# Thirty-six expert steps for thirty-nine: eight of them shared by two experts on two column halves of the array

## The chip, the core and the metric

The kernel runs on one core of one Trainium2 chip. The metric is the device time of the program in microseconds. The engines are named PE (TensorE), DVE (VectorE), ACT (ScalarE), POOL (GpSimd) and SP (SyncE); PEld is TensorE's weight load.

## The reference

Two layers over 4 batches of 512 tokens of 512 numbers (f32). The first quantizes to int8 levels, multiplies, gates and multiplies again, batch by batch, and adds the result to x. The second is a mixture of 8 experts, each token going to the two that its router scores highest:

```python
x = x + _L0_xattn_ref(_layernorm(x, axis=-1), fside_BxS2xS2_0, ctx_1024)
x = x + _L0_ffn_ref(_layernorm(x, axis=-1), L0_ffn_router_w, ...)

scores = jnp.einsum('btd,de->bte', x, router_w)
routing_weights, routing_idx = jax.lax.top_k(jax.nn.softmax(scores, axis=-1), 2)
routing_weights = routing_weights / jnp.sum(routing_weights, axis=-1, keepdims=True)
...
gate = jnp.einsum('bted,edf->btef', dispatched, gate_proj)      # 512 -> 256
up = jnp.einsum('bted,edf->btef', dispatched, up_proj)          # 512 -> 256
act = jax.nn.silu(gate) * up
expert_out = jnp.einsum('btef,efd->bted', act, down_proj)       # 256 -> 512
return jnp.einsum('bted,bte->btd', expert_out, combine_weights)
```

2048 tokens with two picks are 4096 rows for the experts. With the inputs drawn, the reference picks the experts 0 to 7 for 537, 487, 492, 519, 516, 531, 512 and 502 rows.

## The kernel before

The first layer runs batch by batch, its steps interleaved by tables of steps, one table for each engine (`SP_ORDER`, `POOL_ORDER`, `DVE_ORDER`, `ACT_ORDER`, `PE_ORDER`). An engine works its table off strictly in order; semaphores hold it where an operand is missing. Meanwhile the experts' weights are loaded and split into a 16-bit high part and a 16-bit rest ("high" on ScalarE, "low" on GpSimd), and stay on the chip for all eight experts.

The second layer sorts the 4096 rows by expert into tiles of 128 rows. VectorE chooses, ranks and makes one-hot matrices ("choose", "place"); TensorE applies them ("sort", "table"). "list" (`list_tiles`, L907) works out, with small operations that each wait for the one before (`then`, L807), how many tiles each expert owns and where they start; "indices" (`compact` on TensorE L1289, `indices` on VectorE L943) turns this into the rows to gather and to scatter, the expert of each tile and, in `scatter_after`, the number of tiles that must have landed before it. This happens twice: after batches 0 and 1 for nine early tiles that are certainly full (`EARLY`), and after the last batch for the rest (`MOST` = 30). 39 tiles are made because 4096 rows on eight experts can need that many; tiles without a row are computed too.

One expert step i is, by engine:

- GpSimd gathers 128 token rows with an indirect DMA ("gather", L666), four tiles ahead for the late tiles.
- TensorE transposes them ("x low", L1313), ScalarE takes the f16 high part (L1104), VectorE the rest (L970).
- TensorE multiplies with the expert's gate and up weights in three passes: 12 matmuls, cut in two parts of six ("up first", "up rest", L1328). ScalarE applies silu (L1111), VectorE multiplies (L978).
- TensorE transposes again ("a low", L1339), ScalarE and VectorE evict (L1118, L988), TensorE multiplies with the down weights: six matmuls ("take y" on TensorE, L1349), and ScalarE evicts with the row's weight ("take y" on ScalarE, L1133).
- GpSimd adds the 128 rows to the output in memory with an indirect DMA ("scatter", L687).

A matmul of the experts has 128 columns of weights (the tile's rows) and streams 512 numbers of an expert's weights. From step 11 on the orders are made by a loop: on TensorE x low i + 1, up first i, a low i - 1, up rest i, take y i - 1.

A token's two experts are two additions to one row, which must not be in flight together. So a scatter of an early tile waits for the one before (L679). A late one loads `scatter_after`, waits for the semaphore `landed` and does a one-column operation (`hold`, L288): it waits until all tiles of earlier experts have landed, not for those of its own. SP counts `landed` up as the scatters land, in order (L517 to L521). On GpSimd's queue, gather i + 4 stands in front of one scatter, or of two at every third i; scatters 3 to 8 are still to be done when the late part begins. ScalarE's take y i writes into the buffer of tile i - 8 and waits for its landing (L1131).

`keep_busy` (L1164) issues matmuls whose result nobody reads in the first layer; `IN_STRIPS` cuts some of them into two or four column strips of the array.

## Time and profile before

| | us |
|---|---|
| median of three runs | 383.36 |
| the three runs | 381.07, 383.36, 383.91 |
| the profiled execution | 381.06, span 379.3 |
| PE busy / DVE / ACT / POOL | 321.9 / 225.1 / 202.9 / 244.5 |

The span runs from the first to the last instruction of the profiled execution; its own time is 1.76 us more. The granted clock of TensorE was 0.993 of full speed over the span. The late expert steps run from about 223 us on; the last one ends at 370 us, and its rows land after that. Times in the rows are counted from the span's start.

### The profile page before, as it was taken

The numbers are of one execution on the slowest core, as the hardware profiler recorded it, in microseconds if no ns is written. First come the engines' busy times: TensorE is split into PE (matmuls) and PEld (weight loads), VectorE is DVE, ScalarE is ACT, GpSimd is POOL, SyncE is SP. The second block draws the span as 40 slices with busy tenths as digits, with TensorE's granted clock in tenths as the row PEclk, the third lists the DMA queues.
The fourth block names the chain that finished last, engine by engine and source line by source line (L and its number), as shares of the span: only waits on it lengthen the run. The fifth ranks groups of instructions, "written<-read, shape, count | busy, mean of one in ns | idle before, by whom it ended". The sixth has DMA issues, their size and how long they took to land.

```text
span 379.3 us, 6450 instructions
## 1 busy us (share of the span) xinstructions
PE 321.9 (85%) x1955; PEld 189.8 (50%) x1955; DVE 225.1 (59%) x515; ACT 202.9 (54%) x382; POOL 244.5 (64%) x271
## 2 busy tenths in 40 slices
PE   4698757877798885679899899999999999999980
PEld 1455435545665652375574455555555555555530
DVE  3588887879899988878678732333333333333320
ACT  1557568888897796139635234444444444444430
POOL 6486697879999971685461472656667746675441
PEclk9999999999999999999999999999999999999997
DMA  7765446745765508147127554557687657786544
GB/s 247 245 264 196 136 163 199 265 147 165 277 258 188 189 35 242 64 167 232 75 31 275 86 144 80 101 99 116 129 137 115 125 95 123 132 137 107 92 55 55
DMA packets 27551, 56.79 MB, mean 150 GB/s; under 512 B 2624, under 2 KB 13888, under 8 KB 25600
## 3 DMA queue, kind: packets, MB, share of 16 engines
q0 software_dynamic: 8736, 20.45, 29.9%
q1 hardware_dynamic: 17968, 35.39, 27.0%
q10 hardware_dynamic: 816, 0.54, 0.5%
q8 instruction: 18, 0.29, 0.3%
q14 instruction: 13, 0.11, 0.1%
HBM read 37.50 MB, written 18.87 MB: 149 GB/s over the span
## 4 chain that ended last, share of the span: by engine, by line
PE 33%; POOL 22%; issue 17%; DVE 14%; ACT 5%; DMA 4%; POOLq 2%; SPq 0%; DVEq 0%; ACTq 0%
PE bank_h L1328 13%; PE bank_q L1349 6%; POOL x L648 4%; POOL w_in L666 3%; POOL out L687 3%; DVE amax L726 3%; PE bank_t L1313 3%; PE bank_q L1194 2%; POOL w_in L619 2%; POOL gu_lo L584 2%; DVE rmax L756 2%; POOLq L682 2%; PE bank_h L1222 2%; ACT xn L1014 2%; DMA stage<-tokens,gather_at 2%
## 5 line engine op out<-in xcount | busy, mean ns | idle before, releaser
L1328 PE MATMUL bank_h<-gu_hi,xT 128*128 x312 | 103.9, 379 | 0.0
L1328 PE MATMUL bank_h<-gu_lo,xT 128*128 x156 | 59.1, 379 | 0.0
L970 DVE SCALAR_TENSOR_TENSOR xT<-bank_t,xT 128x512 f16<-128x512 f32 x39 | 26.8, 689 | 53.9 <-ACT xT L1104 53.8
L1349 PE MATMUL bank_q<-dn_hi,aT 128*128 x156 | 52.6, 379 | 1.7 <-DVE aT L988 1.4
L1328 PEld LDWEIGHTS bank_h<-gu_hi,xT 128*128 128x128 f16 x312 | 30.5, 98 | 29.3 <-issue 0.2
L666 POOL DMA_INDIRECT w_in<-tokens,gather_at x30 | 29.8, 993 | 17.8 <-issue 7.6
L584 POOL TENSOR_TENSOR gu_lo<-stage,gu_hi 128x1024 bf16<-128x1024 f32 x16 | 34.0, 2135 | 7.5 <-ACT gu_hi L1061 7.3
L978 DVE SCALAR_TENSOR_TENSOR gated<-bank_h,gated 128x256 f32<-128x256 f32 x39 | 16.5, 422 | 32.0 <-ACT gated L1111 32.0
L1111 ACT ACTIVATE gated<-bank_h 128x256 f32<-128x256 f32 x39 | 14.9, 383 | 38.0 <-PE bank_h L1328 38.0
L726 DVE TENSOR_REDUCE amax<-bank_t 128x1 f32<-128x512 f32 x48 | 30.8, 684 | 6.6 <-PE bank_t L1194 4.7
L687 POOL DMA_INDIRECT out<-h,scatter_at x17 | 26.9, 1580 | 11.8 <-DMA out<-h,scatter_at 4.5
L687 POOL DMA_INDIRECT out<-xn,scatter_at x16 | 25.2, 1575 | 11.6 <-ACT xn L1133 9.7
L1349 PE MATMUL bank_q<-dn_lo,aT 128*128 x78 | 29.6, 379 | 0.0
L1118 ACT ACTIVATE aT<-bank_r 128x256 f16<-128x256 f32 x39 | 14.8, 383 | 27.0 <-PE bank_r L1339 25.8
L988 DVE TENSOR_TENSOR aT<-bank_r,aT 128x256 f16<-128x256 f32 x39 | 16.3, 422 | 20.4 <-ACT aT L1118 20.4
L1104 ACT ACTIVATE xT<-bank_t 128x512 f16<-128x512 f32 x39 | 23.0, 591 | 9.2 <-PE bank_t L1313 8.9
L1349 PEld LDWEIGHTS bank_q<-dn_hi,aT 128*128 128x128 f16 x156 | 15.2, 97 | 21.8 <-issue 8.1
L288 POOL TENSOR_TENSOR hold_p<-identf 128x1 f32<-128x1 f32 x30 | 11.1, 372 | 21.0 <-SPq L521 18.5
L648 POOL TENSOR_TENSOR x<-x,xn 128x512 f32<-128x512 f32 x16 | 19.9, 1284 | 4.2 <-DVE xn L802 4.1
L1328 PEld LDWEIGHTS bank_h<-gu_lo,xT 128*128 128x128 f16 x156 | 15.3, 98 | 11.4
L1133 ACT ACTIVATE h<-bank_q,slot_weight 128x512 f32<-128x512 f32 x17 | 11.7, 687 | 15.1 <-PE bank_q L1349 15.1
L619 POOL TENSOR_TENSOR w_in<-w_in,row_s 128x1024 f32<-128x1024 f32 x8 | 17.3, 2184 | 3.0 <-ACT row_s L1027 2.9
(197 smaller groups left out, 704.5 us busy)
## 6 DMA issues: line engine op xcount, KB each, us to landing
stage<-in_L_ffn_gate_proj SPq DMA_DIRECT2D x8, 512.0 KB, 4.2
stage<-in_L_ffn_up_proj SPq DMA_DIRECT2D x8, 512.0 KB, 4.1
stage<-in_L_ffn_down_proj SPq DMA_DIRECT2D x8, 512.0 KB, 4.9
x<-in_x SPq DMA_DIRECT2D x4, 1024.0 KB, 6.3
out<-x SPq DMA_DIRECT2D x4, 1024.0 KB, 4.6
tokens<-xn SPq DMA_DIRECT2D x4, 1024.0 KB, 4.5
x_in<-in_x SPq DMA_DIRECT2D x3, 1024.0 KB, 7.5
w_in<-in_fside_BxS2xS SPq DMA_DIRECT2D x3, 1024.0 KB, 5.6
```

The costliest lines, as they stand in the source:

```text
L584: pool.tensor_tensor(lo, staged(k), hi, ALU.subtract).then_inc(sem("lo_done"), 1)
L619: pool.tensor_tensor(rows, rows, spread(row_s1[:], [P, J // 2, D], 1), ALU.mult).then_inc(sem("ws_ready"), 1)
L648: pool.tensor_tensor(x1[:, j], x1[:, j], xn2[:, j], ALU.add).then_inc(sem("x1_ready"), 1)
L666: pool.indirect_dma_start(out=xg(i), out_offset=None, in_=rows, in_offset=bass.IndirectOffsetOnAxis(ap=gather_at[:, i:i + 1], axis=0)).the ...
L687: pool.indirect_dma_start(out=out, out_offset=bass.IndirectOffsetOnAxis(ap=scatter_at[:, i:i + 1], axis=0), in_=y(i), in_offset=None, comp ...
L726: dve.tensor_reduce(amax[which][:, b % 2, side, c, 0:1], bank, AX.X, ALU.max, apply_absolute_value=True).then_inc(ring_t.taken, 1)
L970: dve.scalar_tensor_tensor(out=xT[i % 2][:, 1].rearrange("p c t -> p (c t)"), in0=bank, scalar=X_SCALE, in1=xT[i % 2][:, 0].rearrange("p c ...
L978: dve.scalar_tensor_tensor(out=gated[i % 2][:], in0=bank[:, F:2 * F], scalar=A_SCALE / X_SCALE, in1=gated[i % 2][:], op0=ALU.mult, op1=ALU ...
L988: dve.tensor_tensor(aT[i % 2][:, 1].rearrange("p c t -> p (c t)"), bank[:, 0:F], aT[i % 2][:, 0].rearrange("p c t -> p (c t)"), ALU.subtra ...
L1104: act.activation(xT[i % 2][:, 0].rearrange("p c t -> p (c t)"), bank, ACT.Copy, scale=X_SCALE).then_inc(sem("x_high"), 1)
L1328: ins = pe.matmul(bank, xT[i % 2][:, part, c], rhs[:, cols], start=(c == 0 and m == 0), stop=(c == C - 1 and m == 2))
L1349: ins = pe.matmul(bank, aT[i % 2][:, part, c], rhs[:, cols], start=(c == 0 and n == 0), stop=(c == FC - 1 and n == 2))
```

## The change

The tiles are now counted in halves of 64 rows. Each expert's rows make `halves` = whole halves (count / 64, rounded down) and a rest of 0 to 63 rows. Two whole halves make a full tile; there are places for 28 of them, 9 early and 19 late (`WHOLE`, `FULL`). Eight mixed tiles, steps 15 to 22 (`MIXED_FROM`), have two halves each. The high half of mixed tile k belongs to expert k and holds its rest. The low half holds expert k's odd whole half, if it has one; otherwise it is free, and the halves of full tiles beyond the 28 are put into the free ones ("spilled"). In all 36 steps.

- TensorE: in a mixed step each of the 18 matmuls becomes two, on 64 columns of weights: the low one with the expert's weights at an address in a register, the high one with expert k's at a fixed address. They write partitions 0 to 63 and 64 to 127 of one bank.
- GpSimd: a mixed tile is scattered in two DMAs of 64 rows. `scatter` of the low half waits until every unit before has landed, by a constant. `scatter_high` loads `high_after` and waits for what `scatter` k waited for, and for the low half also, where that holds a spilled half. Late full tiles behind step 22 wait at least for all mixed units. There are 19 + 16 = 35 late units (`UNITS`); two steps of three take two scatters from the list instead of one of three. The semaphores of the landings are 16 instead of 8.
- VectorE: "list" has three operations more, "indices" one; new are "halves 0" (nine), "mixed list 0" (eleven) and "mixed indices 0" (twelve), and on TensorE "mixed indices 0" (16 small matmuls).
- `share` is one column, broadcast; a few more constants are made at the start by GpSimd.

```diff
+HALF = P // 2
+MIXED_FROM = 15
+FAR = 4096.0
...
 DVE_ORDER
-    "place 2, x low 6, up 5, table 2, list 1, x low 7, indices 1, up 6, a low 4, a low 5, up 7, a low 6, x low 8, "
-    "x low 9, x low 10, up 8, up 9, a low 7, a low 8, up 10, a low 9")
+    "place 2, x low 6, up 5, table 2, list 1, x low 7, indices 1, halves 0, up 6, a low 4, a low 5, mixed list 0, up 7, a low 6, x low 8, "
+    "mixed indices 0, x low 9, x low 10, up 8, up 9, a low 7, a low 8, up 10, a low 9")
 PE_ORDER
-    "indices 1, x low 8, a low 5, up first 7, up rest 7, take y 4, a low 6, take y 5, x low 9, up first 8, "
+    "indices 1, x low 8, a low 5, up first 7, up rest 7, mixed indices 0, take y 4, a low 6, take y 5, x low 9, up first 8, "
...
-    TILES = (N * TOPK + E * (P - 1)) // P
+    MIXED = E
+    WHOLE = (N * TOPK // HALF - MIXED) // 2
+    TILES = WHOLE + MIXED
+    MIXED_END = MIXED_FROM + MIXED
+    UNITS = TILES - EARLY + MIXED
+    FULL = WHOLE - EARLY
+    AHEAD = MIXED_FROM - EARLY
...
-        to_scatter = waiting + [("scatter", i) for i in range(EARLY, TILES)]
+        to_scatter = waiting[:]
+        for i in range(EARLY, TILES):
+            to_scatter.append(("scatter", i))
+            if MIXED_FROM <= i < MIXED_END:
+                to_scatter.append(("scatter high", i))
...
-            for _ in range(2 if to_scatter[0] not in waiting and i % 3 == 0 else 1):
+            for _ in range(2 if to_scatter[0] not in waiting and i % 3 != 1 else 1):
...
+        def units_upto(i):
+            return 1 + i + 1 - EARLY + min(max(i + 1 - MIXED_FROM, 0), MIXED)
+        def unit(i, half=0):
+            return units_upto(i - 1) - 1 + half
...
             def scatter(i):
...
-                    before = pool.value_load(scatter_after[0:1, i:i + 1], min_val=1, max_val=MOST)
+                elif phase == 1:
+                    before = pool.value_load(scatter_after[0:1, i:i + 1], min_val=1, max_val=1 + UNITS)
                     pool.wait_ge(sem("landed"), before)
                     hold(pool, i)
+                else:
+                    pool.wait_ge(sem("landed"), 1 + unit(i))
                 ring_q.emptied(pool, "take y", 0, i)
+                if phase < 2:
+                    add_rows(i, 0, y(i), scatter_at[:, i:i + 1])
+                else:
+                    add_rows(i, 0, y(i)[0:HALF], scatter_at[0:HALF, i:i + 1])
+            def scatter_high(i):
+                k = i - MIXED_FROM
+                before = pool.value_load(high_after[0:1, k:k + 1], min_val=1, max_val=1 + UNITS)
+                pool.wait_ge(sem("landed"), before)
+                hold(pool, i)
+                add_rows(i, 1, y(i)[HALF:P], high_at[0:HALF, k:k + 1])
...
             def gate_up(half, i):
...
+                        if phase_of[i] < 2:
+                            ins = pe.matmul(bank, xT[i % 2][:, part, c], rhs[:, cols], start=start, stop=stop)
+                        else:
+                            pe.matmul(bank[0:HALF], xT[i % 2][:, part, c, 0:HALF], rhs[:, cols], start=start, stop=stop)
+                            own = (gu_hi, gu_lo, gu_hi)[m][:, i - MIXED_FROM, c]
+                            ins = pe.matmul(bank[HALF:P], xT[i % 2][:, part, c, HALF:P], own, start=start, stop=stop)
...
             def take_y(i):
...
-                        act.wait_ge(sem("landed"), before - EARLY + 2)
+                        act.wait_ge(sem("landed"), units_upto(before))
```

On GpSimd's queue (POOL), in the late expert steps, a gather and a scatter stood like this before; `w_in` is the gather's buffer, `h` the scatter's, `[waits ...]` names semaphores:

```order
L666 DMA w_in<-tokens,gather_at 128x512 [waits t_filled]
L682 TENSOR_LOAD scatter_after
L682 ISA x2
L288 TENSOR_TENSOR hold_p<-identf 128x1 [waits landed]
L687 DMA out<-h,scatter_at 7168x512 [waits q_taken]
```

Now, from the gather in front of the low half of step 16 to the one behind its high half:

```order
L707 DMA w_in<-tokens,gather_at 128x512 [waits t_filled]
L713 DMA out<-h,scatter_at 7168x512 [waits q_taken,landed]
L741 TENSOR_LOAD high_after
L741 ISA x2
L314 TENSOR_TENSOR hold_p<-identf 128x1 [waits landed]
L713 DMA out<-h,high_at 7168x512
```

A mixed step puts two scatters into the queue, and the first waits for `landed` itself, with a constant, before the next gather can be issued.

On TensorE (PE), between up rest 7 and take y 4, nothing stood before:

```order
L1328 MATMUL bank_h<-gu_lo,xT 128x512
L1328 MATMUL bank_h<-gu_hi,xT 128x512
L1349 ISA [waits q_taken,x_row_taken]
L1349 MATMUL bank_q<-dn_hi,aT 128x512
```

Now the small matmuls of "mixed indices 0" stand there, and the first waits for VectorE's "mixed list 0" (`halves_listed`):

```order
L1468 MATMUL bank_h<-gu_hi,xT 128x512
L1431 MATMUL bank_r<-low_onehot,table 64x8 [waits halves_listed,w_row_taken]
L1431 MATMUL bank_r<-low_onehot,table 64x8 x5
L1431 MATMUL bank_r<-high_onehot,table 64x8 x6
L1434 MATMUL bank_r<-low_onehot,expert_col 128x8 x2
L1437 MATMUL bank_r<-high_onehot,table 64x8 x2
L1494 ISA [waits q_taken,x_row_taken]
L1494 MATMUL bank_q<-dn_hi,aT 128x512
```

Take y 4 has moved behind a wait for VectorE.

## Rows read from the trace of the kernel before

**Rows 1.** The page: busy time of the engines, and the chain that ended last.

```profile
PE 321.9 (85%) x1955; PEld 189.8 (50%) x1955; DVE 225.1 (59%) x515; ACT 202.9 (54%) x382; POOL 244.5 (64%) x271
...
PE 33%; POOL 22%; issue 17%; DVE 14%; ACT 5%; DMA 4%; POOLq 2%; SPq 0%; DVEq 0%; ACTq 0%
```

**Rows 2.** Busy time by stretches: from:to, length, each engine's, clock, DMA share, GB/s.

```profile
260.00:280.00 20.00, 19.96 (x106) 10.75 (x106) 6.58 (x13) 8.19 (x18) 15.02 (x17) 1.00 0.76 124
280.00:325.00 45.00, 45.00 (x239) 24.21 (x237) 15.39 (x30) 19.38 (x40) 29.19 (x34) 1.00 0.69 119
```

**Rows 3.** Timeline of PE: start, length, engine, line, operation; transposes of tiles 17, 18.

```profile
261.33 0.60 PE L1313 MATMUL bank_t<-identf,w_in 128*128 128x128 f32 x4
...
265.87 0.60 PE L1313 MATMUL bank_t<-identf,w_in 128*128 128x128 f32 x4
```

**Rows 4.** Timeline of POOL: a hold precedes a scatter; in brackets idle time, releaser.

```profile
258.45 0.19 POOL L288 TENSOR_TENSOR hold_p<-identf 128x1 f32<-128x1 f32 x1 [2.27 <-SPq L517]
258.80 1.60 POOL L687 DMA_INDIRECT out<-h,scatter_at  x1 [0.16 <-issue]
...
260.78 1.57 POOL L687 DMA_INDIRECT out<-xn,scatter_at  x1 [0.16 <-issue]
...
265.94 1.01 POOL L666 DMA_INDIRECT w_in<-tokens,gather_at  x1 [0.30 <-issue]
...
267.33 1.58 POOL L687 DMA_INDIRECT out<-xn,scatter_at  x1 [0.16 <-issue]
...
272.97 0.19 POOL L288 TENSOR_TENSOR hold_p<-identf 128x1 f32<-128x1 f32 x1 [2.73 <-SPq L521]
```

**Rows 5.** Waits: who for whom, total us, times, longest.

```profile
POOL hold_p L288 <- SPq L521: 18.5, 7, 3.9
```

**Rows 6.** Timeline of POOL: scatters 7, 8, 28 and the last, 38.

```profile
248.14 1.59 POOL L687 DMA_INDIRECT out<-h,scatter_at  x1 [2.22 <-DMA out<-h,scatter_at]
...
253.31 1.59 POOL L687 DMA_INDIRECT out<-h,scatter_at  x1 [2.30 <-DMA out<-h,scatter_at]
...
330.61 1.58 POOL L687 DMA_INDIRECT out<-xn,scatter_at  x1 [0.15 <-issue]
...
371.01 1.55 POOL L687 DMA_INDIRECT out<-h,scatter_at  x1 [1.34 <-ACT h L1133]
```

**Rows 7.** Timeline of PE: fillers on 64 columns of the array, and the matmul after.

```profile
21.12 6.67 PE L1171 MATMUL bank_q<-number,below 128*64 128x512 f16 x60
...
82.26 1.92 PE L1171 MATMUL bank_h<-number,below 128*64 128x512 f16 x16
84.11 1.04 PE L1222 MATMUL bank_h<-dqT,aqT 128*128 128x512 bf16 x4
```

**Rows 8.** Timelines of DVE, PE and POOL: list 1, indices 1, take y 4; gather 15.

```profile
213.01 0.16 DVE L915 TENSOR_TENSOR count<-base,expert_base 128x8 f32<-128x8 f32 x1
...
215.14 0.30 DVE L931 TENSOR_SCALAR tile_onehot<-tile_number,tile_at,valid 128x30 f16<-128x30 f32 x1
...
215.59 0.23 PE L1298 MATMUL bank_r<-tile_onehot,table 128*128 128x30 f16 x3 [0.50 <-DVE tile_onehot L931]
...
217.52 0.41 DVE L978 SCALAR_TENSOR_TENSOR gated<-bank_h,gated 128x256 f32<-128x256 f32 x1
...
220.00 0.38 PE L1349 MATMUL bank_q<-dn_hi,aT 128*128 x1
...
236.92 0.98 POOL L666 DMA_INDIRECT w_in<-tokens,gather_at  x1 [5.19 <-PE bank_t L1313]
```

**Rows 9.** The page: software DMA queue; and the output's scatters, issue to landing.

```profile
q0 software_dynamic: 8736, 20.45, 29.9%
...
DMA to landing us min/median/max: 3.9/5.0/6.3
```

More of the change, by code:

```diff
@@ L400, in block_kernel @@
         ring_w = Ring(pe_order, [bank_r[:, 1]], sem("w_row_filled"), sem("w_row_taken"),
-                      {"rows 1": 1, "rows 2": 1, "w1 scale row": 1, "sort": 1, "indices": 1}, [("a low", 1)])
+                      {"rows 1": 1, "rows 2": 1, "w1 scale row": 1, "sort": 1, "indices": 1, "mixed indices": 1}, [("a low", 1)])
         ring_q = Ring(pe_order, banks(bank_q), sem("q_filled"), sem("q_taken"),
@@ L517, in _ @@
             sp.sem_inc(sem("landed"), 1)
-            for i in range(EARLY, TILES):
-                n = i - EARLY
-                sp.wait_ge(sem(f"added{n % (2 * J)}"), 16 * (n // (2 * J) + 1))
+            for n in range(UNITS):
+                sp.wait_ge(sem(f"added{n % (4 * J)}"), 16 * (n // (4 * J) + 1))
                 sp.sem_inc(sem("landed"), 1)
@@ L668, in gather, with add_rows @@
                                         ).then_inc(gathered(i), 16)
+            def add_rows(i, half, rows, at):
+                pool.indirect_dma_start(out=out, out_offset=bass.IndirectOffsetOnAxis(ap=at, axis=0), in_=rows, in_offset=None,
+                                        compute_op=ALU.add).then_inc(sem("added") if i < EARLY else sem(f"added{unit(i, half) % (4 * J)}"), 16)
             def scatter(i):
@@ L941, in tiles_done, with list_halves @@
                 then(dve.scalar_tensor_tensor(out=tiles_of[:, 1], in0=left[:], scalar=0.0, in1=tiles_of[:, 0], op0=ALU.max, op1=ALU.min))
+            def list_halves(_):
+                then(dve.tensor_tensor(before_e[:], spread(tiles_of[:, 3], [P, E, E], 1), no_later[:], ALU.mult))
+                then(dve.tensor_reduce(ends[:], before_e[:], AX.X, ALU.add))
+                then(dve.tensor_tensor(left[:], expert_number[:], ends[:], ALU.subtract))
+                then(dve.scalar_tensor_tensor(out=free_at[:], in0=tiles_of[:, 3], scalar=FAR, in1=left[:], op0=ALU.mult, op1=ALU.add))
+                then(dve.tensor_reduce(spilled[:], tiles_of[:, 0], AX.X, ALU.add))
+                then(dve.tensor_scalar(spilled[:], spilled[:], 2.0, -2.0 * FULL, ALU.mult, ALU.add))
+                for half in range(2):
+                    then(dve.tensor_scalar(low_at[:, half:half + 1], tile_at[:], 2.0, half - 2.0 * FULL, ALU.mult, ALU.add))
+                then(dve.tensor_scalar(beyond[:], tile_at[:], float(FULL), valid[:, 1:2], ALU.is_ge, ALU.mult))
@@ L992, in _ @@
                     {"centre": centre, "choose": choose, "place": place, "table": add_to_table, "list": list_tiles, **({"done": tiles_done} if EARLY else {}),
+                     "halves": list_halves, "mixed list": mark_halves, "mixed indices": mixed_indices,
                      "indices": indices, "x low": x_low, "up": up, "a low": a_low,
@@ L1261, in rank @@
                     pe.wait_ge(sem("base_ready"), g)
-                pe.matmul(rank, share[:], spread(base[g][:], [P, m + 1, E], 1), start=True, stop=False)
+                pe.matmul(rank, share[:].to_broadcast([P, P]), spread(base[g][:], [P, m + 1, E], 1), start=True, stop=False)
                 pe.wait_ge(sem("mask_ready"), g + 1)
@@ L1301, in compact, with compact_halves @@
                           stop=True).then_inc(ring_w.filled, 1)
+            def compact_halves(_):
+                bank = ring_w.fill(pe, "mixed indices", 0, 0)
+                ring_w.emptied(pe, "sort", 0, len(GROUPS) - 1)
+                pe.wait_ge(sem("halves_listed"), 1)
+                for half, onehots in enumerate((low_onehot, high_onehot)):
+                    for v in range(3):
+                        for n in range(2):
+                            pe.matmul(bank[half * HALF:(half + 1) * HALF, v * MIXED:(v + 1) * MIXED],
+                                      table[:, v, n * HALF:(n + 1) * HALF], onehots[:, n], start=(n == 0), stop=(n == 1))
+                for n in range(2):
+                    pe.matmul(bank[:, 3 * MIXED:4 * MIXED], expert_col[:].to_broadcast([P, P]), low_onehot[:, n],
+                              start=(n == 0), stop=(n == 1))
+                for n in range(2):
+                    ins = pe.matmul(bank[0:HALF, 4 * MIXED:5 * MIXED], table[:, 0, n * HALF:(n + 1) * HALF], high_onehot[:, n],
+                                    start=(n == 0), stop=(n == 1))
+                ins.then_inc(ring_w.filled, 1)
             experts = {}
```

126 lines of the change are left out of this document (97 added, 29 removed).

## The prediction

> **What bounds the kernel now.** I read the page first. TensorE has matmuls in flight for 85% of the span, GpSimd is busy for 64% [rows 1]. The chain of work that ended last speaks against taking TensorE for the only limit: 22% of it lies on POOL, 17% is "issue", and after 280 us it hardly touches a matmul [rows 1]. Then the busy time by stretches. From 260 to 325 us, well inside the late expert steps, TensorE is full at a granted clock of 1.00 (2.4 GHz), and POOL is at 15.0 of 20 and 29.2 of 45 us, with DMA engines at 0.76 and 0.69 [rows 2]. A step costs TensorE 4.54 us between the transposes of two tiles [rows 3]: 18 matmuls of 512 columns and six transposes.
>
> The third view is POOL's timeline [rows 4]. It prices the queue that one engine works off in order: a gather costs 1.31 us (1.01 busy, 0.30 idle before it), a gather and its scatter 3.27 to 3.28, a second scatter right behind one 1.97 (258.80 to 260.78). Where an expert changes, the hold waits for the scatter before to land: 267.33 to 272.97 is 5.64, and the scatter follows 0.34 later. Such a wait idles 2.2 to 3.9 us, seven of them 18.5 us [rows 5]. Nearly unloaded, with only a gather behind each scatter, a landing costs 5.17 and 5.14 us from start to release (248.14, 253.31, 258.45) [rows 4, 6]. I use 5.3 for a landing and 5.67 from scatter to scatter across one.
>
> These prices replay the kernel before. Scatter 9 starts at 258.80; up to scatter 28 the order has 4 scatters right behind another (7.9), 9 behind a gather (29.4) and 6 landings (at the experts' first tiles 13, 16, 19, 22, 25, 28: 34.0). That gives 330.1; the row says 330.61 [rows 4, 6]. So POOL sets its own pace in this stretch and has only about half a microsecond a step to spare against 4.54: what is added there lands on the path.
>
> **TensorE, steps.** Three full steps fewer: 3 x 4.54 = -13.6. A mixed step issues 36 matmuls of 64 columns of weights for 18 of 128. Whether two column halves run at once the trace shows: 60 filler matmuls on 64 columns take 6.67 us, 0.22 a pair, as much as one full matmul [rows 7]. So the pairs cost nothing more. Changing between the forms does: 16 half fillers (8 pairs, 1.72) start at 82.26, the next full matmul at 84.11, 0.13 later than 8 pairs explain [rows 7]. A mixed step changes four times: 8 x 4 x 0.13 = +4.2. Bounds: the fillers stream one shared operand, the mixed halves two different ones, so from nothing more to 8 x 3.9 = +31 if they took turns; I take the row.
>
> **VectorE's lists.** Small list operations take 0.21 us each (213.01 to 215.14, ten of them) [rows 8]. Before take y 4 TensorE now has to pass "mixed indices 0", which waits for "mixed list 0" on VectorE. In front of its release stand 3 + 1 + 9 + 8 = 21 new operations, 4.4 us. VectorE was through with a low 5 at about 218.6 (217.52 plus three short evictions), so the release comes at 223.0. TensorE went on at 220.00 [rows 8]; it now stalls 2.4 us after its own 0.6 of delay, then runs 16 small matmuls (three took 0.23 in their group [rows 8]; 0.9 with two changes of form): take y 4 starts near 224.0, +4.0. The 12 operations of "mixed indices 0" then stand before x low 9 on VectorE and hold up first 9 by some 0.3 more. Sum +4.3, bounds +2 (if the evictions slip in earlier) and +5. POOL inherits it in full: its gather 15 waited 5.19 us for TensorE's transposes, until 236.92 [rows 8]. The initial iotas and selects gain five short ones; POOL idles 2.1 us behind them, they cost nothing.
>
> TensorE's own end moves by -13.6 + 4.2 + 4.3 = -5.1.
>
> **POOL, scatters.** A mixed step scatters twice, 64 rows each. The low half waits for every earlier unit to have landed; the high half follows at once, but also waits for its low half where that holds a spilled tile. Queued behind each wait are the gathers, and behind these TensorE's next tiles; ScalarE's take y waits for the landing eight tiles back. Which wait applies follows from the picks of the reference's inputs: experts get 537, 487, 492, 519, 516, 531, 512, 502 rows. In whole 64-row halves that is 8, 7, 7, 8, 8, 8, 8, 7; 29 full tiles against 28 places, so one spills, into the low halves of steps 15 and 18. The same counts give the places of the waits before (13, 16, 19, ...), which the replay confirmed.
>
> Prices of a half: its issue is between 1.97 (nothing saved) and 1.18 (half of the 1.58 busy saved); I take 1.57. Its landing: the software queue keeps the DMA engines for 29.9% of 379.3 us over 39 gathers and 39 scatters, 1.45 each [rows 9]; half of that, 0.73, goes, and half the issue saving, 0.4: 5.3 - 1.1 = 4.2. Bounds: 3.6 (5.1 less 0.73 and 0.79) and 5.3.
>
> - Start of scatter 9: 258.80 + 4.3 = 263.1.
> - To low 15: one scatter right behind, one behind a gather, wait (12), one right behind, wait (14), wait (15): 1.97 + 3.27 + 5.67 + 1.97 + 5.67 + 5.3 = 23.9; 287.0.
> - Low 15 to scatter 23: six steps of 1.57 + 4.2 = 34.6; two spilled ones of 4.2 + 0.35 + 4.2 = 17.5; two gathers between a low and its high 2.6; sum 54.7 and 0.35 for the last hold: 55.1; 342.1. Bounds 46.4 and 68.1.
> - To scatter 35: waits before 24, 26, 28, 30, 34, seven right behind: 28.4 + 13.8 = 42.1; 384.2.
> - The last scatter before starts at 371.01, the span ends 8.29 later [rows 6]: 392.5.
>
> So +13.2 on the span, although TensorE's own work would end earlier: 381.06 + 13.2 = **394.3 us** by the profiled execution. That execution is the fastest of the three (median 383.36), so the median may be up to 2 higher; I say **394**.
>
> The Trainium skill ("DMA: Bandwidth & Descriptors", Anatomy of one DMA) gives a GpSimd DMA as about 2.0 us plus bytes / 436 GB/s, most of the fixed part waiting for the write's receipt. By that a half's landing would save only 0.30 us; as an estimate from the page, with no issue saved either, the mixed stretch would be 65 us and the time 404. The forecast goes by the rows.
>
> **Rivals.**
> - *A half lands like a whole.* Nothing saved: low 15 to scatter 23 is 68.1, the time 407. For it: the landings differ little under light and heavy load (5.1 to 5.6) [rows 4, 6]. Chance 0.10. The page just named points this way.
> - *Halves are cheap and TensorE stays the bound: faster.* POOL may lag at first and catch up as long as landing and issue of a half stay near 2.8 + 1.0; then 381.06 - 5.1 = 376. At 3.2 + 1.0 it draws level. For it: the shortest whole landing is 3.9 of a median 5.0 [rows 9], and 3.9 - 0.73 = 3.2. Against: that one is the extreme, and 5.1 holds in the early, lightly loaded chain. Chance 0.12. This is the one on the other side.
> - *The column halves take turns.* TensorE's end, 5.1 earlier by the sum, comes 31 later instead: 381.06 - 5.1 + 31 = 407. Against: the fillers' 0.22 a pair. Chance 0.05.
> - *The waits are milder.* The kernel's own router puts one pick otherwise (expert 6 has exactly 512 rows), nothing spills (two waits less, -6.0), or VectorE's lists cost 2: about 386, no change. Chance 0.13.
> - *Forecast*, POOL's chain of landings: 0.60, from 386 (the bounds' lower corner) to 401 (landing 4.6, nothing saved on the issue).
>
> What this kernel's measurement tells from no change is about 1%, 3.8 us, so 379.5 to 387.2 counts as the same. Faster 0.12 (second rival); same 0.14 (the fourth, and the forecast's low corner); slower 0.74. The range that holds 8 in 10: 383 to 404, leaving out the fast rival and the worst corners.
>
> **What would show it.** In the profile after: gaps between matmuls of up to some 3 us from step 25 on, before the transposes (POOL's gathers late); waits of holds and scatters on SP or DMA some 17 to 19 instead of 8 in the late phase; low-to-low distances in steps 16 to 22 of 5.3 to 6.4, and 8.5 to 9.5 at 15 and 18; the matmuls of the mixed steps 0.22 a pair; TensorE idle about 2.4 us before its small matmuls at 223; a last scatter at about 384. It is wrong if half scatters follow each other at under 4.6 a step, if the mixed steps take over 7 us of TensorE without a wait, or if the last scatter still waits for its own take y.

## The result, and the profile after

The changed kernel takes **399.06 us** (median of four runs, 396.02 to 402.31), the kernel before 383.28 in the runs beside it: 1.040 times as long, 95% interval 1.032 to 1.047. The ratios, here and below, leave out executions more than 1.5% above the fastest of their kernel (402.31 here, one of e3, two each of e10 and e11); the medians hold all of them. The profiled execution is the fastest, 396.02 us with a span of 394.3, 15.0 more than before. The direction and the mechanism are as forecast. The size is too small by a third of the change: 394 was forecast, 10.6 us above the median before, and 15.8 were measured. The section on the prediction says which terms were right and which only cancelled.

The page of the changed kernel: busy times, the chain that ended last, the software queue.

```profile
PE 322.0 (82%) x2020; PEld 186.2 (47%) x2043; DVE 227.1 (58%) x543; ACT 197.5 (50%) x370; POOL 246.8 (63%) x275
...
POOL 29%; issue 22%; PE 20%; DVE 15%; ACT 5%; DMA 4%; POOLq 3%; SPq 0%; DVEq 0%; ACTq 0%
...
q0 software_dynamic: 8192, 18.88, 26.8%
```

TensorE's busy time is as before [rows 1], though three steps are gone. Stretches at a lower granted clock (0.83 in 140 to 160 us, 0.94 in 350 to 380) are a part of that; how large a part was not worked out. The chain that ended last has moved from TensorE (20% for 33%) to POOL (29% for 22%) and "issue" (22% for 17%).

Busy time by stretches; columns as in [rows 2].

```profile
280.00:325.00 45.00, 43.16 (x302) 21.91 (x305) 13.22 (x27) 17.68 (x36) 24.27 (x25) 1.00 0.50 85
310.00:350.00 40.00, 35.90 (x177) 18.92 (x180) 11.61 (x24) 14.56 (x30) 25.07 (x26) 0.96 0.50 90
350.00:380.00 30.00, 22.27 (x102) 10.73 (x102) 6.18 (x13) 9.25 (x18) 19.04 (x21) 0.94 0.67 96
```

From 280 on TensorE has gaps, and POOL is at 25 of 40 us in 310 to 350. Neither is full. What fills POOL's time is in its timeline, here scatter 14 and steps 15 to 17, then the high half of step 19 and the low half of step 20; `scatter_at` is a low half, `high_at` a high one.

```profile
284.36 1.58 POOL L713 DMA_INDIRECT out<-h,scatter_at  x1 [0.15 <-issue]
290.03 1.44 POOL L713 DMA_INDIRECT out<-h,scatter_at  x1 [4.10 <-SPq L559]
...
293.89 0.19 POOL L314 TENSOR_TENSOR hold_p<-identf 128x1 f32<-128x1 f32 x1 [1.10 <-SPq L559]
294.23 1.45 POOL L713 DMA_INDIRECT out<-h,high_at  x1 [0.16 <-issue]
...
298.23 1.45 POOL L713 DMA_INDIRECT out<-h,scatter_at  x1 [1.23 <-SPq L559]
...
300.06 1.43 POOL L713 DMA_INDIRECT out<-h,high_at  x1 [0.16 <-issue]
...
304.07 1.44 POOL L713 DMA_INDIRECT out<-h,scatter_at  x1 [1.28 <-SPq L559]
...
305.90 1.42 POOL L713 DMA_INDIRECT out<-h,high_at  x1 [0.16 <-issue]
...
321.38 1.47 POOL L713 DMA_INDIRECT out<-xn,high_at  x1 [0.16 <-issue]
325.43 1.42 POOL L713 DMA_INDIRECT out<-xn,scatter_at  x1 [2.58 <-SPq L559]
```

Read it as pairs. 294.23 to 298.23: the high half of step 15 lands 4.00 after its start, and the next low half starts in that moment. 298.23 to 300.06: a high half right behind its low one, 1.83. The high half of step 16 lands 4.01 later (300.06 to 304.07), so a step is 1.83 + 4.01 = 5.84. In step 15 the high half also waits for its low half, which holds a spilled tile (290.03 to 293.89, 3.86): 8.20 from low to low, and 8.11 in step 18. In steps 19 and 20 a gather stands between low and high. The waits in the late part:

```profile
POOL hold_p L314 <- SPq L559: 22.8, 10, 4.3
...
POOL out L713 <- SPq L559: 15.4, 8, 4.1
...
PE bank_t L1451 <- DMA w_in<-tokens,gather_at: 9.1, 5, 2.9
```

That makes eighteen waits for a landing that SP counts (line 559), 38 us, where there were seven and 18.5 [rows 5]. The third row is new: five times TensorE waits for a gather, up to 2.9 us, because the gather stood behind a landing on POOL's queue. ScalarE's take y, which waits for the landing eight tiles back, was held up once, for 1.0 us.

### The profile page after: what moved, and what is told of

It is laid out like the page before. It is cut to its first block, busy times and chain, and to the rows that moved or that the text cites. A ratio compares the mean times of both kernels' runs of the same rounds, so it can differ in the third digit from the quotient of the medians.

```text
span 394.3 us, 6561 instructions
## 1 busy us (share of the span) xinstructions
PE 322.0 (82%) x2020; PEld 186.2 (47%) x2043; DVE 227.1 (58%) x543; ACT 197.5 (50%) x370; POOL 246.8 (63%) x275
## 4 chain that ended last, share of the span: by engine, by line
POOL 29%; issue 22%; PE 20%; DVE 15%; ACT 5%; DMA 4%; POOLq 3%; SPq 0%; DVEq 0%; ACTq 0%
POOL out L713 8%; PE bank_h L1468 6%; POOL w_in L707 5%; POOL x L689 4%; DVE amax L782 3%; PE bank_q L1494 3%; PE bank_q L1314 2%; POOL w_in L660 2%; POOL gu_lo L625 2%; DVE rmax L812 2%; POOLq L727 2%; PE bank_r L1404 2%; ACT xn L1134 1%; DMA stage<-tokens,gather_at 1%; PE bank_h L1342 1%
## 5 line engine op out<-in xcount | busy, mean ns | idle before, releaser
L1468 PE MATMUL bank_h<-gu_hi,xT 128*128 x224 | 77.5, 395 | 0.5
L1468 PE MATMUL bank_h<-gu_lo,xT 128*128 x102 | 40.2, 394 | 0.0
L1494 PE MATMUL bank_q<-dn_hi,aT 128*128 x112 | 37.8, 379 | 2.0 <-DVE aT L1107 1.4
L1468 PEld LDWEIGHTS bank_h<-gu_hi,xT 128*128 128x128 f16 x224 | 22.6, 101 | 23.3 <-issue 3.5
L713 POOL DMA_INDIRECT out<-xn,scatter_at x14 | 21.5, 1533 | 9.3 <-SPq L559 7.8
L1451 PE MATMUL bank_t<-identf,w_in 128*128 128x128 f32 x108 | 16.9, 279 | 9.5 <-DMA w_in<-tokens,gather_at 9.1
L1472 PE MATMUL bank_h<-gu_hi,xT 128*64 128x512 f16 x64 | 22.0, 385 | 0.0
L1470 PE MATMUL bank_h<-gu_hi,xT 128*64 x64 | 22.0, 385 | 0.0
L1451 PEld LDWEIGHTS bank_t<-identf,w_in 128*128 128x128 f32 x108 | 12.2, 141 | 18.6 <-issue 16.4
L672 POOL TENSOR_TENSOR av<-h 128x512 f32<-128x512 f32 x8 | 10.0, 1270 | 15.1 <-PE bank_q L1314 12.1
```

The lines of the kernel that those rows point to most:

```text
L713: pool.indirect_dma_start(out=out, out_offset=bass.IndirectOffsetOnAxis(ap=at, axis=0), in_=rows, in_offset=None, compute_op=ALU.add).then ...
L1451: ins = pe.transpose(bank[:, c * P:(c + 1) * P], xg(i)[:, c * P:(c + 1) * P], identf[:])
L1468: ins = pe.matmul(bank, xT[i % 2][:, part, c], rhs[:, cols], start=start, stop=stop)
L1470: pe.matmul(bank[0:HALF], xT[i % 2][:, part, c, 0:HALF], rhs[:, cols], start=start, stop=stop)
L1472: ins = pe.matmul(bank[HALF:P], xT[i % 2][:, part, c, HALF:P], own, start=start, stop=stop)
L1494: ins = pe.matmul(bank, aT[i % 2][:, part, c], rhs[:, cols], start=start, stop=stop)
```

## Where the 15 us went

| start of | before | after | later by |
|---|---|---|---|
| take y 4 (TensorE) | 220.00 | 225.87 | 5.9 |
| gather 15 (POOL) | 236.92 | 243.31 | 6.4 |
| scatter 9 | 258.80 | 265.69 | 6.9 |
| last scatter | 371.01 | 385.82 | 14.8 |

So 6.9 us are lost before the first late scatter, and 7.9 behind it, although there are three tiles fewer. 1.66 of the 6.9 stand before the lists begin: VectorE and ScalarE agree to 0.04 us up to 141 us, then TensorE's granted clock is 0.83 in 140 to 160 (1.00 before), and "list 1" starts at 214.67 for 213.01. The runs do not point at the change for that: e2, with the changed kernel's steps in that stretch, has 1.00 there, and e1, with those of the kernel before, 0.91. The profile before is also an unusually fast one, at 0.993 over the span where 55 other runs of that kernel have 0.968 to 0.987. In e1, whose steps up to the late scatters are those of the kernel before, the matmuls of indices 1 come at 219.37 for 215.59. So a difference of a few us in the starting times of two profiles need not be the change. From list 1 on, the two profiles part by the lists. Their two places on TensorE:

```profile
218.06 0.23 PE L1418 MATMUL bank_r<-tile_onehot,table 128*128 128x27 f16 x3 [1.31 <-DVE tile_onehot L992]
...
219.93 0.63 PE L1468 MATMUL bank_h<-gu_hi,xT 128*128 x1
...
225.23 0.23 PE L1431 MATMUL bank_r<-low_onehot,table 128*64 128x8 f16 x3 [1.28 <-DVE low_onehot L1027]
...
225.87 0.39 PE L1494 MATMUL bank_q<-dn_hi,aT 128*128 x1
...
228.69 0.60 PE L1451 MATMUL bank_t<-identf,w_in 128*128 128x128 f32 x4
```

TensorE waits 1.31 us for list 1 (0.50 before [rows 8]) and 1.28 for the mixed list. Between them the matmul at 219.93 takes 0.63 instead of 0.38: the clock has fallen to its lower level, 1.2 GHz, as the stretch shows (0.50 of full speed).

```profile
219.90:222.10 2.20, 2.20 (x8) 0.79 (x6) 1.86 (x13) 0.87 (x2) 1.66 (x2) 0.50 0.17 37
```

## The experiments

The median of each kernel's runs, and the ratio to the runs of the kernel before beside it. e2 and what is built on it (e6, e7, e10, e11) scatter both halves of a mixed tile in one DMA. A token that stands in both halves of step 15 or 18 is then added twice in one DMA, and the order of these additions is left out. These kernels price a step of the argument; they are not finished kernels.

| kernel | median us | ratio, 95% interval |
|---|---|---|
| e1 before, landings one by one | 391.2 | 1.021 [1.019, 1.023] |
| e2 one scatter for a mixed tile | 394.3 | 1.029 [1.026, 1.032] |
| e3 mixed steps with whole matmuls | 399.3 | 1.035 [1.030, 1.040] |
| e4 lists later | 395.6 | 1.037 [1.030, 1.043] |
| e5 no scatters of mixed tiles | 382.1 | 0.996 [0.993, 0.999] |
| e6 e2, pairs at every fourth i | 392.0 | 1.024 [1.020, 1.027] |
| e7 e6 and lists later | 388.6 | 1.012 [1.008, 1.016] |
| e8 half matmuls apart | 399.3 | 1.042 [1.035, 1.050] |
| e9 changed kernel with fillers | 399.6 | 1.045 [1.042, 1.048] |
| e10 e7, pairs placed by hand | 384.5 | 1.003 [1.000, 1.007] |
| e11 e10 with fillers | 383.4 | 1.000 [0.997, 1.003] |
| e12 e10 with half scatters | 395.0 | 1.031 [1.027, 1.035] |

### Is it the chain of landings?

**e1**, in the kernel *before*, gives nine tiles a wait for all tiles before them:

```diff
-                    before = pool.value_load(scatter_after[0:1, i:i + 1], min_val=1, max_val=MOST)
-                    pool.wait_ge(sem("landed"), before)
-                    hold(pool, i)
+                    if 15 <= i < 24:
+                        pool.wait_ge(sem("landed"), i - EARLY + 1)
+                    else:
+                        ...
```

> The kernel before (39 full tiles, no half scatters, no new list, TensorE untouched), in which the scatters of tiles 15 to 23 wait, by a constant, for every earlier tile to have landed, as the low halves of the mixed steps do. That adds 6 landing waits (15, 17, 18, 20, 21, 23) to the 3 that were there. Theory (the chain of landings on GpSimd's queue decides): each added wait turns 1.97 or 3.27 us from scatter to scatter into 5.67, some 16 to 19 us on the queue, of which the slack at its end (13.8 us by the replay, less what late gathers take from TensorE) gives part back: 390 to 397 us. Rival (the loss comes from column halves, the lists or TensorE's changes of form): 383, no change.

391.2. The waits alone, with no mixed tile, make +8. The theory had the sum on the queue too high: from scatter 9 to 23 POOL takes 62.3 us for 52.1, 10.3 more and not 16 to 19, because a link costs 5.0 to 5.2, not 5.67, and the three waits that were there shrank too (5.6 to 5.8 before). Most of the 10.3 reaches the end, so the queue had little slack. These are whole scatters that wait for one another, in POOL's timeline of e1:

```profile
284.27 1.57 POOL L690 DMA_INDIRECT out<-h,scatter_at  x1 [2.54 <-SPq L521]
...
289.47 1.56 POOL L690 DMA_INDIRECT out<-h,scatter_at  x1 [2.32 <-SPq L521]
...
294.45 1.56 POOL L690 DMA_INDIRECT out<-h,scatter_at  x1 [2.11 <-SPq L521]
...
299.49 1.55 POOL L690 DMA_INDIRECT out<-xn,scatter_at  x1 [3.48 <-SPq L521]
```

They are 5.0 to 5.2 from start to start, 0.4 to 0.7 more than TensorE needs for a step (4.54 [rows 3]).

**e5** takes the chain out and leaves all of TensorE's work in:

```diff
-    UNITS = TILES - EARLY + MIXED
+    UNITS = TILES - EARLY - MIXED
...
-            to_scatter.append(("scatter", i))
+            if not MIXED_FROM <= i < MIXED_END:
+                to_scatter.append(("scatter", i))
...
```

The pairs of scatters are back at every third i, and the late full tiles wait for full tiles alone.

> The changed kernel without the 16 half scatters of the mixed tiles and without the landings counted for them (the eight mixed tiles are gathered and computed, their rows are never added to the output; the late full tiles wait only for full tiles). Theory (GpSimd's chain of landings in steps 15 to 22 sets the end): the chain is gone, TensorE sets the end with its own steps. The last scatter before was at 371.01; three steps less 13.6, form changes +4.2, the start of the late part +5.9 (take y 4, as measured in the changed kernel): 367.5, so about 377.5 us by the whole program, 375 to 381, some 20 below the changed kernel and below the kernel before. No wait of TensorE for a gather after 250. Rival (the mixed steps themselves are slow on TensorE, ScalarE or VectorE, and GpSimd only follows): stays at 390 or more, with waits between engines other than GpSimd.

382.1: 17 below the changed kernel. Without the mixed scatters and their landings the loss is gone. The run takes out 16 issues as well as the waits; that the waits alone cost time is what e1 shows. But 377.5 was expected. TensorE's first transposes of x low 9 and the last ones of all, in the profile of e5 (384.9 us, the slowest of its ten runs):

```profile
233.96 0.77 PE L1447 MATMUL bank_t<-identf,w_in 128*128 128x128 f32 x4
...
361.29 0.63 PE L1447 MATMUL bank_t<-identf,w_in 128*128 128x128 f32 x4 [0.20 <-issue]
```

x low 9 comes 11.2 later than in the kernel before (222.81). From there to the last x low TensorE needs 127.3 us for 135.2 (to 358.02), 7.9 less where 9.4 were expected, and from there to the last scatter 0.9 more, since now the last expert's first tile waits for a landing. Of the 11.2 us, 4.8 are there already at the matmuls of indices 1 (220.38 for 215.59), and of these only 0.8 is the longer wait for list 1; e1 is 3.8 late there without any change. The expectation also started from the fastest execution before, 381.06: from the median, 383.2, the same sum gives 379.7, and the two misses of 1.5 and 0.9 make it 382.1, as measured; that it fits so closely is partly luck, since the start was not 5.9 but 11.2 later in this profile. So in this kernel the late start eats most of what three steps save: by the medians, 1.1 us is left of it.

### Is it the split matmuls?

**e3** issues the mixed steps as whole matmuls, all rows with the low half's expert, and scatters as the changed kernel does:

```diff
-                        if phase_of[i] < 2:
+                        if True:
...
```

> The changed kernel, whose mixed steps use the low half's expert for all 128 rows, in 18 full matmuls as in a full step; the high halves' experts are left out. All scatters and waits as in the changed kernel. A mixed step costs TensorE 4.54 us instead of 5.09. Theory (GpSimd's landings): the tiles are only ready earlier in front of a queue that is late, 399 plus or minus 1.5 us. Rival (TensorE's steps are on the path): 8 x 0.55 less, 394.5.

399.3: no change clear of the spread (ratio 1.035 for 1.040, the intervals overlap), where the rival wanted 4.5 us. Each mixed step does cost TensorE 0.5 less. TensorE loses the saving again in waits: 15.0 us for gathers, seven times, where the changed kernel has 9.1.

**e8** issues the low matmuls of a part first and then the high ones:

```diff
-                            pe.matmul(bank[0:HALF], xT[i % 2][:, part, c, 0:HALF], rhs[:, cols], start=start, stop=stop)
-                            own = (gu_hi, gu_lo, gu_hi)[m][:, i - MIXED_FROM, c]
-                            ins = pe.matmul(bank[HALF:P], xT[i % 2][:, part, c, HALF:P], own, start=start, stop=stop)
+                            ins = pe.matmul(bank[0:HALF], xT[i % 2][:, part, c, 0:HALF], rhs[:, cols], start=start, stop=stop)
...
+                if phase_of[i] == 2:
+                    for c in range(half * C // 2, (half + 1) * C // 2):
+                        for m, part in enumerate((0, 0, 1)):
+                            ...
+                            ins = pe.matmul(bank[HALF:P], xT[i % 2][:, part, c, HALF:P], own,
+                                            start=c == 0 and m == 0, stop=c == C - 1 and m == 2)
```

> The changed kernel, where in a mixed step the low halves' matmuls of a part are all issued first and the high ones' behind them, instead of in turn. Everything else as it is. If two column halves only run at once when their matmuls stand next to each other: a mixed step takes TensorE 36 x 0.22 = 7.9 us of expert matmuls instead of 4.0 in pairs, less three of four changes' worth of nothing; 8.9 to 9.2 a step instead of 5.1, over GpSimd's 6.75 a step, so 8 x 2.3 = 18 later: 408 to 420. If a half's matmul runs at once with the other's whatever stands between (the queue overlaps them anyway): 396 to 402, no change. The same run prices the rival of the prediction, halves that take turns (407).

399.3: no change. What happened lies between the two sides. TensorE's timeline of the changed kernel, and then of e8:

```profile
268.23 0.40 PE L1470 MATMUL bank_h<-gu_hi,xT 128*64 x1
268.23 0.40 PE L1472 MATMUL bank_h<-gu_hi,xT 128*64 128x512 f16 x1
268.47 0.38 PE L1470 MATMUL bank_h<-gu_lo,xT 128*64 x1
268.47 0.38 PE L1472 MATMUL bank_h<-gu_lo,xT 128*64 128x512 bf16 x1
```

```profile
274.37 0.40 PE L1470 MATMUL bank_h<-gu_hi,xT 128*64 x1
274.61 0.38 PE L1470 MATMUL bank_h<-gu_lo,xT 128*64 x1
274.83 0.38 PE L1470 MATMUL bank_h<-gu_hi,xT 128*64 x1
274.83 0.40 PE L1475 MATMUL bank_h<-gu_hi,xT 128*64 128x512 f16 x1
275.05 0.38 PE L1470 MATMUL bank_h<-gu_hi,xT 128*64 x1
```

In the changed kernel both halves of a pair start together. In e8 six low matmuls (L1470) stand before the first high one (L1475), and yet that starts with the third low one: it overtakes three low ones. The step grows from 5.09 to 6.00 us (277.54 to 283.54), not to 9, and 6.00 still hides behind POOL's 6.75 (54.0 us for eight steps). So e8 does not price the rival in which the halves take turns. What rules that rival out is the trace of the changed kernel: the pairs start together, and a mixed step takes 5.09.

### Is it the lists?

**e4** moves the mixed list behind x low 9 on VectorE, and mixed indices 0 behind up rest 10 on TensorE:

```diff
 DVE_ORDER
-    "place 2, ..., indices 1, halves 0, up 6, a low 4, a low 5, mixed list 0, up 7, a low 6, x low 8, mixed indices 0, x low 9, x low 10, ..."
+    "place 2, ..., indices 1, up 6, a low 4, a low 5, up 7, a low 6, x low 8, x low 9, halves 0, mixed list 0, x low 10, up 8, up 9, a low 7, a low 8, mixed indices 0, ..."
...
```

> The changed kernel with halves 0 and mixed list 0 moved on VectorE behind x low 9, and mixed indices 0 moved behind up rest 10 on TensorE and behind a low 8 on VectorE, so that neither stands before take y 4, up 8 or x low 9. Theory (TensorE's stall at 224 us moves GpSimd's whole queue): take y 4 starts 3 to 4 us earlier, scatter 9 too, and the time falls by as much: 395 to 396.5 us. Rival (the queue's own waits absorb it): 399, no change.

395.6. In the profiles x low 9 comes at 226.43 for 228.69, but gather 15 at 242.34 for 243.31 and the last scatter at 384.74 for 385.82: of 2.3 us on TensorE, 1.0 to 1.1 reach POOL's queue. The median gained 3.5, but the two intervals overlap; e7 below shows the gain more clearly.

**e9** fills the two gaps on TensorE with matmuls that nobody reads:

```diff
+    ("indices", 1): 6, ("mixed indices", 0): 12,
...
+                keep_busy(bank, "indices", phase)
                 pe.wait_ge(sem("tiles_listed"), phase + 1)
...
+                keep_busy(bank, "mixed indices", 0)
                 pe.wait_ge(sem("halves_listed"), 1)
```

> The changed kernel with 6 matmuls whose result nobody reads in front of the matmuls of indices 1 on TensorE, and 12 in front of those of mixed indices 0, where TensorE idles 1.3 and 1.3 to 3.0 us for VectorE's lists. Theory (the two gaps let TensorE's granted clock fall to half for some 2.6 to 5 us right behind them; in the profile of e8 it was 226.5 to 231.7, and the tile behind came 3.3 later than in the profile of the changed kernel): the clock stays at 1.00 from 215 to 235, x low 9 comes at about 228, and the median falls from 399 by 2 to 4, to 395 to 397. Rival (the clock falls for another reason, or the late queue swallows it): 398 to 400.

399.6, not the 395 to 397 of its theory: the remedy fails. The clock did stay at 1.00 from 215 to 235 us. But from the first small matmul of indices 1 to x low 9 e9 takes 11.4 us (219.78 to 231.22), the changed kernel's profile 10.6 with the clock falling in the first gap, and e3 and e8 12.2 and 13.5 with the clock falling in the second. The twelve fillers end at 227.8, after the mixed list is ready (VectorE's last operation: 226.74 for 0.17), so a part of what they save is spent on them; the median shows nothing of the rest.

### What do the halves of the scatters cost, and what does the queue's order?

**e2** scatters a mixed tile in one DMA of 128 rows, which waits for all units before it:

```diff
-    UNITS = TILES - EARLY + MIXED
+    UNITS = TILES - EARLY
...
-            for _ in range(2 if to_scatter[0] not in waiting and i % 3 != 1 else 1):
+            for _ in range(2 if to_scatter[0] not in waiting and i % 3 == 0 else 1):
...
-                    add_rows(i, 0, y(i)[0:HALF], scatter_at[0:HALF, i:i + 1])
+                add_rows(i, 0, y(i), scatter_at[:, i:i + 1])
```

> The changed kernel with one scatter of 128 rows for a mixed tile instead of two of 64 (8 DMAs, 8 loads and holds and the two waits between a low and its high half fewer; 27 units; two scatters from the list at every third i as before). A row that stands in both halves of step 15 or 18 is then added twice in one DMA, so the order of these few additions is left out. Theory: low 15 to scatter 23 takes 8 landings of 5.3 to 5.65, 43 to 46 us instead of 54.0; of these 9 to 11 us the tail gives a part back, because the gathers stand differently between the waits: 389 to 397 us. Rival (TensorE's mixed steps bound it): 399, no change.

394.3. Low 15 to scatter 23 fell to 41.3 us from 54.0, yet behind it the profile lost 9: 50.8 to the last scatter for 41.8, and scatter 33 had to wait 4.82 for its take y. TensorE waited 12.2 us for gathers. **e6** takes pairs of scatters at every fourth i (`i % 4 == 0`), and **e7** is e6 with e4's orders:

> As e2_one_scatter (one scatter of 128 rows for a mixed tile), but the loop that makes GpSimd's order takes two scatters at every fourth i, not at every third: the scatters stay one or two tiles further behind the gathers, so that a gather stands less often behind a scatter that waits for its own take y. Theory (in e2 the saving of the mixed stretch was given back because scatters had caught up with ScalarE's take y and held the gathers): the waits of TensorE for gathers, 12.2 us in e2, fall below 6, scatter 23 stays about 41 us behind low 15, the last 12 scatters take 42 to 46 instead of 50.8: 386 to 391. Rival (the tail is bound by its own landings, whatever stands where): 393 to 396, as e2.

> e6_one_scatter_fourth together with e4_lists_later (halves 0 and mixed list 0 behind x low 9 on VectorE, mixed indices 0 behind up rest 10 on TensorE). Theory (POOL's queue sets the pace, and the queue starts its late part with gather 15, which waits for TensorE's transposes): e4 was worth 1 us in the profiles and 3.5 in the medians, the same here on top of e6: 384 to 389. It would still not beat the kernel before by 1%: the late landings are 14 (8 in the mixed steps) against 8. Rival (the two gains overlap, since the queue waits elsewhere): within 1 us of e6.

e6 takes 392.0 (its theory said 391 at most, and waits for gathers under 6 us; they are 6.8), e7 388.6: the lists are worth 3.4 here, and these intervals do not overlap. e7's queue, POOL's timeline at its pair of tiles 15 and 16, shows what is left:

```profile
286.65 1.02 POOL L705 DMA_INDIRECT w_in<-tokens,gather_at  x1 [0.31 <-issue]
290.29 1.57 POOL L711 DMA_INDIRECT out<-h,scatter_at  x1 [2.62 <-SPq L557]
295.21 1.55 POOL L711 DMA_INDIRECT out<-h,scatter_at  x1 [3.36 <-SPq L557]
297.07 1.01 POOL L705 DMA_INDIRECT w_in<-tokens,gather_at  x1 [0.30 <-issue]
```

From gather to gather are 10.4 us with two landings between, and TensorE waits 3.9 for it. **e10** puts the pairs where the second scatter waits for nothing, **e11** adds six fillers in front of indices 1. The diff is against e7:

```diff
+TWO_SCATTERS = (16, 17, 28, 29, 30, 31)
...
-            for _ in range(2 if to_scatter[0] not in waiting and i % 4 == 0 else 1):
+            for _ in range(2 if i in TWO_SCATTERS else 1):
```

> e7_both_fourth (one scatter of 128 rows for a mixed tile, lists later), but the six places where two scatters follow each other without a gather are chosen by hand: tiles 10 and 11, 12 and 13, 24 and 25, 26 and 27, 28 and 29, 30 and 31, whose second one waits for no landing (same expert). In e7 they fell on 15/16 and 20/21 too, where the gap between two gathers was 10.4 us and TensorE waited 7.4 for them. Theory (GpSimd's queue, gathers behind landings): at most 2 us of such waits are left, the rest falls on the end: 382 to 386. Rival (the landings alone bind, 14 of them): 388, as e7.

> e10_scatters_placed with the 6 unread matmuls in front of indices 1 (mixed indices 0 has no gap there any more). Theory of the clock: half clock behind indices 1 cost 1.3 us in the profiles of the changed kernel and e4; 1 to 2 us below e10: 381 to 385, about the time of the kernel before, though TensorE has 9.4 us less of expert steps; what is left is the start of the late part (lists +3 to 4) and the last landing wait (scatter 34 behind 33, where the kernel before has three tiles without rows at its end). Rival: no difference to e10.

e10 takes 384.5, within its 382 to 386, and e11 383.4. The mixed stretch is as long as in e7 (41.6 us for 41.7) but TensorE waits 4.8 for gathers, not 7.4 (2 were expected). e11 takes no longer than the kernel before, and does not beat it, though it leaves an order out. The fillers' own effect, 1.1, is not resolved (the intervals overlap). **e12** is e10 with the scatters split again. Of its diff against e10 only the places of the pairs are shown; the rest puts the half scatters and their waits back:

```diff
-TWO_SCATTERS = (16, 17, 28, 29, 30, 31)
+TWO_SCATTERS = (16, 17, 19, 20, 21, 22, 23, 24, 25, 26, 28, 29, 30, 31)
...
```

> e10_scatters_placed with the half scatters back: lists later, two scatters of 64 rows for a mixed tile right behind each other with no gather between, and the other pairs where e10 has them. It tells how much of the changed kernel's 16 us is the splitting of the scatters itself, and how much the order of the queue and the lists. Theory (each mixed step has one landing in any case; a half's costs 3.95 for 5.15, but its partner's issue of 1.83 comes on top, and the spilled halves of steps 15 and 18 make two landings more): low 15 to scatter 23 is 8 x 5.8 + 2 x 2.2 = 51 for e10's 41.6, about 9 of it at the end: 391 to 395. Rival (the splitting costs little, the gathers between the halves and the crowded places were the loss): 384 to 388.

395.0, at the top of its 391 to 395 and 10.5 above e10. POOL's timeline of one step of the chain, first in e10, then in e12:

```profile
295.10 1.57 POOL L712 DMA_INDIRECT out<-h,scatter_at  x1 [2.22 <-SPq L558]
296.98 1.01 POOL L706 DMA_INDIRECT w_in<-tokens,gather_at  x1 [0.30 <-issue]
300.28 1.57 POOL L712 DMA_INDIRECT out<-h,scatter_at  x1 [2.30 <-SPq L558]
```

```profile
296.44 1.46 POOL L714 DMA_INDIRECT out<-h,scatter_at  x1 [1.30 <-SPq L560]
...
298.28 1.43 POOL L714 DMA_INDIRECT out<-h,high_at  x1 [0.16 <-issue]
300.01 1.00 POOL L708 DMA_INDIRECT w_in<-tokens,gather_at  x1 [0.30 <-issue]
302.29 1.45 POOL L714 DMA_INDIRECT out<-h,scatter_at  x1 [1.29 <-SPq L560]
```

A step takes 5.18 in e10 and 5.85 in e12, and e12 has two more landings for the spilled halves of steps 15 and 18. Low 15 to scatter 23 is 41.6 us in e10 and 52.2 in e12. So the 15.8 us of the changed kernel divide, by the medians, into 4.0 for the lists and the order of the queue (399.1 to 395.0), 10.5 for the splitting of the scatters, with the order that it keeps for the spilled halves (395.0 to 384.5), and 1.2 for the rest (384.5 against 383.3).

## Why the prediction was right, step by step

- **Bound.** POOL's queue of landings and not TensorE: right. Without the mixed scatters the loss is gone (e5), waits alone bring half of it into the kernel before (e1), and e3 and e8 change TensorE's mixed steps by -0.5 and +0.9 us each and move the median by nothing clear of its spread. The reading that POOL "has only about half a microsecond a step to spare" was too low for the stretch that it was taken from: 330.61 - 258.80 is 71.8 us for 19 scatters, 3.78 each, 0.76 below 4.54.
- **TensorE, steps.** A mixed step of 4.54 + 4 x 0.13 = 5.06: measured 5.09 (272.72, 277.81, 282.89). Pairs of different operands cost nothing more than the fillers' pairs.
- **VectorE's lists.** Take y 4 was forecast 4.0 later. It came 5.87 later, 4.2 without the 1.66 that are there before the lists. The sum was right for another reason, which is luck. The small matmuls came at 225.23 for 223.0 (1.66 of it from before the lists). TensorE reached them late itself, at half clock, so it stalled 1.28 there for the forecast 2.4, and 0.8 more at list 1, which the forecast had left out. What POOL inherits was mis-sized: gather 15 came 6.39 later and scatter 9 6.89, without the 1.66 4.7 and 5.2, for the forecast 4.3.
- **To low 15.** 24.3 us, forecast 23.9.
- **Half scatters.** The sum was right by two errors against each other. The issue was taken at 1.57 from half to half and measured 1.83, since the busy time fell by only 0.14 (1.44 for 1.58). The landing was taken at 4.2 and measured 3.95 (3.8 to 4.3 in ten). The spilled steps were taken at 8.75 and measured 8.2 and 8.1. Together 54.0, forecast 55.1.
- **The page's rule.** The Trainium skill ("DMA: Bandwidth & Descriptors", Anatomy of one DMA) would let a half save 0.30 us of a landing. The trace does not agree: a half lands in 3.95 from start to release for 5.15 of a whole one in the same place of the queue (e10), 1.2 less. Its mixed stretch of 65 us, which also had no issue saved, was 11 us too long.
- **To the last scatter, and the end.** 41.8 us, forecast 42.1, and 8.5, forecast 8.3.
- **The rival on the other side** (TensorE stays the bound, 376) fails twice. A half's landing and issue are 3.95 + 1.83 = 5.8, above the 4.2 at which it draws level and also above the 5.09 of a mixed step. And e5 shows that without any mixed scatter the time would be 382, not 376: by the medians 1.1 us is left of the "-5.1". That term is mis-sized, and the fast rival rested on it; the forecast did not.
- **Median against profile.** The median lies 3.0 above the profiled execution, 5.1 above the forecast. 2.3 of the 5.1 were on the table when the forecast was made: it was worked out from the profiled execution before, 381.06, whose median is 383.36, and of "up to 2 higher" nothing was added to 394.3. Profile against profile, 13.2 were forecast and 15.0 measured, and 1.66 of the 1.8 between them stand before the lists. As to why the changed kernel's median lies above its profile, a likely part is the clock behind the stall at mixed indices 0. In five profiles (e2, e3, e5, e6, e8) TensorE reached it at full clock and stood 2.9 us; in four of them the clock fell behind it, and from the small matmuls to x low 9 passed 4.9 to 6.4 us for 3.5 in e2 and in the changed kernel. The changed kernel's one profile is thus a lucky one at this place. But e9, which keeps the clock up, has the same median, so the cause stays open.

## What to carry to other kernels

Where additions to memory must not overlap, count the landings on the path first, and not bytes: in this kernel, halving a scatter turns one landing and one issue into one landing and two issues, and every spilled half adds a landing. Before removing steps of the engine that is full, work out the time per step of the in-order queue beside it, here 5.2 against 4.54. Put a wait where nothing that feeds the full engine stands behind it: the order of that queue alone made 388.6 or 384.5 us of the same work (e7, e10). List operations of 0.2 us each are cheap only where no stage of the main engine waits behind them: moving them gained 3.4 us (e6, e7).

## What the runs showed of the hardware

- **A matmul on the other 64 columns can start before earlier ones.** In e8 the first high matmul of a gate and up part, seventh in the program, started with the third low one, in each part of the three steps from 266 to 284 us. Twelve half matmuls of a part took 1.88 us up to the transposes behind them (272.13 to 274.01); as six pairs they take 1.41 in the changed kernel (268.23 to 269.64), and one after the other they would take 12 x 0.22 = 2.6.
- **An indirect scatter's time follows its rows only in part.** 64 rows for 128: busy on POOL 1.44 for 1.58 us; start to release 3.95 for 5.15.
- **The clock can fall behind a short stall, and does not in every execution.** This is a stretch of e8 behind 2.96 us of idle time of TensorE; the granted clock is 0.50, the lower level:

```profile
226.50:231.70 5.20, 5.20 (x16) 2.17 (x16) 1.51 (x7) 0.96 (x2) 0.00 (x0) 0.50 0.11 39
```

It fell behind the gap of 2.9 us in four profiles of five (e3, e5, e6, e8, not e2), and behind the smaller one (1.3 to 1.4 us at indices 1) in three of ten (the changed kernel, e4, e7). With both filled it stayed at 1.00 in the one profile there is (e9, 215 to 235 us), also in e11 with the gap at indices 1 filled and the other one moved away, and in the profile of the kernel before, with 0.50 us at indices 1, too.
